# Spreading the source numbers of cold edge chunks by a DMA instead of TensorE, in a four-layer graph kernel

## The reference, cut to what matters

```
x = layernorm(x + segment_sum(w * x[src], dst) @ W0.T)
x = layernorm(x + L1(x))     # two convolutions by degree, batch norms, a product over the joined features
x = layernorm(x + L2(x))     # weighted sums again, two dense products
x = layernorm(x + L3(x))     # a convolution by degree
```

## Time and profile before

| | |
|---|---|
| runs, median (lowest to highest) | 3463.71 us (3461.14 to 3464.36) |
| profiled execution: span | 3458.8 us |
| profiled execution: its own time | not given apart from the span; 4.9 us below the median |
| busy over the span: PE, DVE, ACT, POOL | 82%, 57%, 37%, 71% |
| the first stage, by the first and last POOL scatter of line 1701 | 45.3 to 1256.7 us (starts) |

### The profile page before, as it was taken

The page is one execution under the profiler, slowest core; times in us unless marked ns, Lnnn a source line. Parts: engine busy times, 40 slices in busy tenths (PEclk is TensorE's granted clock), DMA queues, the critical chain, the costliest instruction groups (busy, mean ns, idle before and its releaser), DMA issues. The chain is left out here.

```text
span 3458.8 us, 60258 instructions
## 1 busy us (share of the span) xinstructions
PE 2842.7 (82%) x19203; PEld 2100.9 (61%) x19220; DVE 1983.2 (57%) x6763; ACT 1275.6 (37%) x3485; POOL 2462.4 (71%) x2238
## 2 busy tenths in 40 slices
PE   5989877878888859789977997778888875699995
PEld 4777655656666648444446774366666764466664
DVE  7889777777787729442243434443444564245557
ACT  5566666776877739200010002500111232001123
POOL 3888777786676667577747776777777774777773
PEclk8999998999999979899978997589999998799996
DMA  8787788888888879678856886755556564988884
GB/s 273 112 147 113 142 154 148 155 155 170 179 175 170 180 175 354 180 213 231 237 141 177 226 224 172 217 172 158 162 176 181 159 178 124 297 235 247 252 251 137
DMA packets 658436, 652.79 MB, mean 189 GB/s; under 512 B 87902, under 2 KB 606476, under 8 KB 656588
## 3 DMA queue, kind: packets, MB, share of 16 engines
q0 software_dynamic: 153600, 258.41, 37.3%
q1 hardware_dynamic: 430670, 331.83, 31.2%
q10 hardware_dynamic: 73854, 58.70, 5.4%
HBM read 434.19 MB, written 214.52 MB: 188 GB/s over the span
## 5 line engine op out<-in xcount | busy, mean ns | idle before, releaser
L1701 POOL DMA_INDIRECT A<-rows_buf,big x572 | 902.4, 1578 | 333.8 <-issue 143.5
L882 POOL DMA_INDIRECT rows_buf<-T,idx x888 | 847.7, 955 | 275.9 <-issue 272.2
L976 PE MATMUL PSA<-S,rows_buf 128*128 128x128 bf16 (+2 forms) x5904 | 582.5, 254 | 213.9 <-DMA rows_buf<-X,idx 103.5
L976 PEld LDWEIGHTS PSA<-S,rows_buf 128*128 128x128 bf16 (+2 forms) x5904 | 523.3, 142 | 296.8 <-DMA rows_buf<-X,idx 88.0
L882 POOL DMA_INDIRECT rows_buf<-X,idx x528 | 509.5, 965 | 160.9 <-issue 157.8
L1032 DVE TENSOR_TENSOR accT<-PSA,accT 128x256 f32 (+2 forms) x354 | 132.8, 375 | 835.7 <-PE PSA L976 828.5
L1556 DVE TENSOR_TENSOR accT<-PSA,accT 128x392 f32 (+5 forms) x366 | 239.7, 655 | 173.0 <-issue 59.6
L1394 PE MATMUL PSA<-XRS,rows_buf 128*128 128x256 f32 x1144 | 313.0, 398 | 6.4 <-ACT rows_buf L1406 6.4
L793 ACT ACTIVATE accT<-accT,vec 128x500 f32<-128x500 f32 (+3 forms) x26 | 17.7, 693 | 666.5 <-DVE accT L791 666.4
L1406 ACT ACTIVATE rows_buf<-PSA 128x512 f32<-128x512 f32 x286 | 168.0, 593 | 186.1 <-PE PSA L1394 175.8
L1394 PEld LDWEIGHTS PSA<-XRS,rows_buf 128*128 128x128 f32 x1144 | 209.8, 197 | 32.0 <-ACT rows_buf L1385 6.8
(11 more groups left out here) (315 smaller groups left out, 5805.3 us busy)
## 6 DMA issues: line engine op xcount, KB each, us to landing
XRS<-Ad SPq DMA_DIRECT2D x400, 256.0 KB
Ad<-accT SPq DMA_DIRECT2D x224, 196.0 KB
XRS<-in_xpad SPq DMA_DIRECT2D x192, 128.0 KB, 3.3
Awd<-accT SPq DMA_DIRECT2D x48, 392.0 KB, 3.6
A<-accT SPq DMA_DIRECT2D x9, 1600.0 KB
rows_buf<-T,idx POOLq DMA_INDIRECT x888
rows_buf<-A SPq DMA_DIRECT2D x24, 512.0 KB
accT<-A SPq DMA_DIRECT2D x24, 512.0 KB, 6.1
```

Of the source, the lines that this page charges most:

```text
L882: s_hg[slot(i)][j // 2].on(pool.indirect_dma_start(Gv(slot(i), j), None, table, bass.IndirectOffsetOnAxis(idx[:, c:c + 1], 0)), 16)
L976: last = pe.matmul(PS[bank_of(i)][0:F, W * h:W * h + W], Gv(slot(i), j)[:, o:o + F], hits[:, i % SRING, j, :], start=j + part == 0, stop=j ...
L1701: s_k[n].on(pool.indirect_dma_start(A, bass.IndirectOffsetOnAxis(tgt[:, c:c + 1], 0), G[:, i % RING, j, :], None, compute_op=ALU.add), 16)
```

## The change

The source numbers of each group come as one row of 512 int32 from a new DRAM input `srcrow`, and SP loads it into all 128 partitions with a broadcast transfer (128 times 2 KB). It goes to a ring of three buffers `SR` (SRB = 3), taken from the buffer `junk`, from the space of `srch` and `srcl`, and from the tensor W3, whose weights are loaded after the cold steps. The first three loads are issued after all `zero_copy`; the others stand first in SP's step, three steps ahead, behind a wait for the `equals` that frees the buffer. `equals` does, per chunk, one `scalar_tensor_tensor` that compares, multiplies by `upto` (a bf16 triangle with its diagonal) and writes the row sum. PE's `source_rows`, ACT's `row_sums` and DVE's line 1338 are gone, as are four preparing DVE instructions (lines 439 to 442) and two POOL ones. DVE's `targets(i + 1)` is placed in the middle of step i for all steps.

```diff
-FAR = 16384
+SRB = 3
-    pool.tensor_copy(identb[:, :], ident[:, :])
-    pool.tensor_scalar(lowerb[:, :], lower[:, :], float(FAR), None, ALU.mult)
+    pool.tensor_tensor(upto[:, :], lower[:, :], ident[:, :], ALU.add)
-    link(v.tensor_scalar(tmpi, idx[:, :], 63, None, ALU.bitwise_and))
-    link(v.tensor_copy(srcl, tmpi))
-    link(v.tensor_tensor(tmpi, idx[:, :], tmpi, ALU.subtract))
-    link(v.tensor_copy(srch, tmpi))
...
+        def load_src(i):
+            if i >= SRB:
+                sp.wait_ge(s_eq, i - SRB + 1)
+            g = G0 + i
+            sp.dma_start(SR[i % SRB], a["srcrow"][g:g + 1, :].broadcast_to([128, CG * 128])).then_inc(s_srb[i % SRB], 16)
...
         def transfers(p):
+            if SRB <= p + 1 < NCOLD:
+                load_src(p + 1)
             if 4 <= p < NCOLD:
                 load_x(p)
...
-            v.wait_ge(s_sr, i + 1)
-            v.tensor_tensor(Eq[:, i % 2, :, :], PS[0].rearrange("p (j e) -> p j e", j=CG),
-                            srcf[:, g, :].unsqueeze(2).broadcast_to([128, CG, 128]), ALU.is_equal).then_inc(s_eq, 1)
+            v.wait_ge(s_srb[i % SRB], 16 * (i // SRB + 1))
+            for j in range(CG):
+                last = v.scalar_tensor_tensor(Eq[:, i % 2, j, :], SR[i % SRB][:, 128 * j:128 * j + 128], srcf[:, g, j:j + 1], upto,
+                                              ALU.is_equal, ALU.mult, accum_out=cnt[:, g, j:j + 1])
+            last.then_inc(s_eq, 1)
...
         s_q.by(sp)
         for e in (sc, pool):
             s_cst.by(e)
+        for i in range(SRB):
+            load_src(i)
         transfers(0)
         transfers(1)
-        source_rows(0)
-        source_rows(1)
         weigh(0)
-        row_sums(0)
...
-            if i + 2 < NCOLD:
-                source_rows(i + 2)
...
-            if i + 1 < NCOLD:
-                row_sums(i + 1)
...
+        s_cst.by(v)
         equals(0)
         hot_hits(0)
         scatter_rows()
+        targets(0)
         for i in range(NCOLD):
...
-            if i <= BYACT:
-                targets(i)
...
-            if BYACT < i + 1 < NCOLD:
+            if i + 1 < NCOLD:
                 targets(i + 1)
...
+        sp.wait_ge(s_eq, NCOLD)
+        s_w.on(sp.dma_start(W3[:, :, :], halves(a["L3_gnn_W"])), 16)
```

More of the change, by code:

```diff
@@ L1299, in transfers @@
                     dense_load(sp, t)
[L1301 to L1310, removed]
         def equals(i):
@@ L1316, in equals @@
             v.tensor_tensor(Su[:, i % 2, :, :], iota4, cur16[:, g:g + 1, :].broadcast_to([128, W, CG]), ALU.is_equal).then_inc(s_su, 1)
-            v.wait_ge(s_sr, i + 1)
-            v.tensor_tensor(Eq[:, i % 2, :, :], PS[0].rearrange("p (j e) -> p j e", j=CG),
-                            srcf[:, g, :].unsqueeze(2).broadcast_to([128, CG, 128]), ALU.is_equal).then_inc(s_eq, 1)
[L1321 to L1327, removed]
+            v.wait_ge(s_srb[i % SRB], 16 * (i // SRB + 1))
[3 more added lines that the diff above has]
+            last.then_inc(s_eq, 1)
         def targets(i):
             g = G0 + i
[L1332 to L1337, removed]
-                    last = v.tensor_tensor_reduce(out=junk[:, j, :], in0=Eq[:, i % 2, j, :], in1=lower[:, :], scale=1.0, scalar=0.0,
-                                                  op0=ALU.mult, op1=ALU.add, accum_out=cnt[:, g, j:j + 1])
-                last.then_inc(s_cn, 1)
-                v.wait_ge(s_cn, i + i - BYACT + 1)
-                least = 0.0
-            v.scalar_tensor_tensor(cnt[:, g, :], cnt[:, g, :], least, spare[:, g, :], ALU.is_gt, ALU.mult).then_inc(s_cn, 1)
-            v.wait_ge(s_cn, i + 1 + max(0, i - BYACT + 1))
+            v.wait_ge(s_eq, i + 1)
+            v.scalar_tensor_tensor(cnt[:, g, :], cnt[:, g, :], 1.0, spare[:, g, :], ALU.is_gt, ALU.mult).then_inc(s_cn, 1)
+            v.wait_ge(s_cn, i + 1)
             v.tensor_tensor(tgt[:, CG * g:CG * g + CG], cnt[:, g, :], srcA[:, g, :], ALU.add).then_inc(s_b, 1)
@@ L1845, in spread @@
             sp.dma_start(XR[:, 0, :], a["xpad"][bass.ds(lo, 128), :]).then_inc(s_x[0], 16)
-            pe.wait_ge(s_staged, 1)
+            turned_at = nc.values_load_multi_w_load_instructions(
+                ctl[0:1, 3:4], engines=[ET.SP], min_val=0, max_val=NG - 1, skip_runtime_bounds_check_because="held under NG")[1][0]
+            sp.dma_start(SR[0], a["srcrow"][bass.ds(turned_at, 1), :].broadcast_to([128, CG * 128])).then_inc(s_srb[0], 16)
+            v.wait_ge(s_srb[0], 16)
             for j in range(CG):
-                o = PS[0][:, 128 * j:128 * j + 128]
-                pe.matmul(o, f_h[:, j:j + 1].broadcast_to([128, 128]), identb[:, :], start=True, stop=False)
-                last = pe.matmul(o, f_l[:, j:j + 1].broadcast_to([128, 128]), identb[:, :], start=False, stop=True)
-            last.then_inc(s_sr, 1)
-            v.wait_ge(s_sr, 1)
-            v.tensor_tensor(Eq[:, 0, :, :], PS[0].rearrange("p (j e) -> p j e", j=CG),
-                            f_src.unsqueeze(2).broadcast_to([128, CG, 128]), ALU.is_equal).then_inc(s_eq, 1)
+                last = v.scalar_tensor_tensor(Eq[:, 0, j, :], SR[0][:, 128 * j:128 * j + 128], f_src[:, j:j + 1], upto,
+                                              ALU.is_equal, ALU.mult, accum_out=f_cnt[:, j:j + 1])
+            last.then_inc(s_eq, 1)
             v.wait_ge(s_eq, 1)
-            for j in range(CG):
-                last = v.tensor_tensor_reduce(out=junk[:, j, :], in0=Eq[:, 0, j, :], in1=lower[:, :], scale=1.0, scalar=0.0,
-                                              op0=ALU.mult, op1=ALU.add, accum_out=f_cnt[:, j:j + 1])
-            last.then_inc(s_cn, 1)
+            v.scalar_tensor_tensor(f_cnt, f_cnt, 1.0, f_spare, ALU.is_gt, ALU.mult).then_inc(s_cn, 1)
             v.wait_ge(s_cn, 1)
-            v.scalar_tensor_tensor(f_cnt, f_cnt, 0.0, f_spare, ALU.is_gt, ALU.mult).then_inc(s_cn, 1)
-            v.wait_ge(s_cn, 2)
             v.tensor_tensor(f_tgt, f_cnt, f_srcA, ALU.add).then_inc(s_turn_b, 1)
@@ L1934, in build @@
     s_aw = [nc.alloc_semaphore(f"s_aw{i}") for i in range(2)]
-    s_rs = nc.alloc_semaphore("s_rs")
+    s_srb = [nc.alloc_semaphore(f"s_srb{i}") for i in range(SRB)]
     ABW = [XS[:, 2 + i, :].bitcast(BF16) for i in range(2)]
-    junkA = XS[:, 0:2, :].rearrange("p a b -> p (a b)").rearrange("p (j e) -> p j e", j=CG)
     Eq = Z[:, 0:4, :].rearrange("p a b -> p (a b)").rearrange("p (r j e) -> p r j e", r=2, j=CG)
     Ms = Z[:, 4:8, :].rearrange("p a b -> p (a b)").rearrange("p (r n) -> p r n", r=2)
-    junk = Z[:, 8:10, :].rearrange("p a b -> p (a b)").rearrange("p (j e) -> p j e", j=CG)
+    SR = [ap.bitcast(I32) for ap in (Z[:, 8:10, :].rearrange("p a b -> p (a b)"), part[4][:, 0:512], W3[:, :, :].rearrange("p k n -> p (k n)"))]
     spread()
@@ L2379, in by_chunk @@
         return full.reshape(n, 128).T
+    given["srcrow"] = np.concatenate([given["src"], np.zeros(128 * NG * CG - E, given["src"].dtype)]).reshape(NG, 128 * CG)
     given["src"] = by_chunk(given["src"], NG * CG, 0)
```

28 lines of the change are left out of this document (10 added, 18 removed).

## The result

The changed kernel takes 3530.14 us (median of 4 runs, 3526.07 to 3539.01), the kernel before, run beside it, 3462.43 us (3458.26 to 3464.36): a ratio of 1.0207 [1.0193, 1.0222]. It is slower by some 68 us; the prediction said 3461 and at most 3507. The profiled execution took 3539.01 us, its span is 3537.8.

What follows compares the result with a forecast made beforehand. It took the first stage as bound by PE early, mutual DVE and PE waits in the middle, and SP's window parts late. Terms +30 - 10 - 13 - 9 made -2: 3461 us as a run, no tellable change; range 3424 to 3507.

Steps and rivals of the forecast that it cites:

- Part 1, the start: Start of first stage: the first source row lands behind the zeroing, so step 4's tables come 30 us late (28 to 34).
- Part 2, the compare: DVE, each step: four compares with row sums take 0.87 us instead of 0.60, +0.27; net -0.69 in the last 51 steps.
- The rival with the dear compare (1.3 us): DVE, steps 4 to 93: four compares at 1.3 us cost 0.7 per step, kernel 3491 us; chance 0.07.
- Part 3, PE: PE, each step: twelve matmuls go, saving 0.67 us.
- part 4, ACT: ACT, 92 steps: four row sums go, 1.2 us per step, and with them DVE's 13.0 us of waits for them.
- the -10 of steps 4 to 22: PE-bound steps 4 to 22: 18 steps at 0.67 us less some given back by DVE's +0.27, a gain of 10 us.
- Part 5, SP and the DMA engines: 143 loads of 256 KB cost SP about 1.0 us per step (0.4 to 2.3); slower scatters cost nothing while POOL has slack.
- -9 in the last stretch: Steps 94 to 142: 46 loads add 46 us to SP's occupied time, so 415 us against 424, a gain of 9.
- the formula of the prediction: Last stretch, SP-bound: it takes 364 + 5 + 46c us, c being SP's us per step for a load.
- SP's queue is the price: Last stretch: loads standing before window parts in SP's step cost c = 2.0 us each, +37, kernel 3507 us; chance 0.20.

Runs made afterwards that it cites:

- e1: The changed kernel with its first three source loads issued before the zeroing instead of behind it; ratio 1.0099 to the kernel before.
- e11: The kernel of e9 with each of DVE's four compare-and-count instructions issued twice, the copies unread; ratio 1.0237 to the kernel before.
- e9: The changed kernel without source loads in the cold steps: PE makes the rows in two matmuls a chunk, DVE compares from PSUM; 3441.06 us, ratio 0.9942.
- e10: The kernel of e9 with ACT's four row sums put back, unread, in the first 92 steps, and DVE's wait for them; ratio 1.0213.
- e8: The kernel of e9 with the first matmul of each chunk issued twice, so twelve matmuls a step again; ratio 0.9999 to the kernel before.
- e2: The changed kernel with the loads from the fourth on issued by ACT's queue at the end of its step; ratio 1.0196 to the kernel before.
- e7: The kernel of e9 with the 256 KB loads put back on SP's queue at their place, read by nobody; ratio 1.0141 to the kernel before.
- e12: The kernel of e7 with the unread loads ended at step 93; ratio 0.9991 to the kernel before.
- e5: The changed kernel unaltered, run again as a yardstick; 3532.5 us, ratio 1.0217 to the kernel before.
- e3: The changed kernel with int16 source rows, 128 KB a load in the same number of packets; ratio 1.0087 to the kernel before.
- e6: The changed kernel with the first three loads ahead of the zeroing and int16 source rows; ratio 1.0041 to the kernel before.

## Why the prediction was wrong

The sum was +30 - 10 - 13 - 9 = -2; the profiled spans gave +79.0. The miss of 81 us is 4 at the start, 27 in steps 4 to 93, 53 in the last stretch, and -3 behind it.

**Part 1, the start: right.** +34.0 at the end of its range (28 to 34), by the mechanism given: first compare at 62.44 (61 to 63 foreseen) behind a wait of 40.03. e1 takes 24 us of it back.

**Part 2, the compare: mis-sized.** 1.09 us for the four, not 0.87; the pitch is 0.27, not the 0.21 of line 1338. The term is +0.49 a step, not +0.27, and e11 shows that DVE's time counts up to step 94, in full from step 22 on. The prediction let a good part of it be hidden by waits for PE. 0.22 by 90 steps is 20 us of the 27 by which steps 4 to 93 missed their forecast; the loads' 8.5 to 10 us (below) are of the size of the rest. The rival with the dear compare (1.3 us) was no nearer than the forecast: 1.09 lies 0.21 below the one and 0.22 above the other. The rule of the Trainium skill that stood with it ("Vector Engine (DVE) Microarchitecture Reference", section 7, half rate with two sources in SBUF that are not bf16) has no case here: 345 ns from SBUF with int32 and 344 from PSUM with f32 in e9. The Trainium skill, the same page, section 5.2, gives one column a cycle, 1.0417 ns, and some 75 ns for each instruction; from that I estimate 0.21 us for 128 columns. The row sums of line 1338 kept to it; this instruction with its accumulator takes 0.06 more.

**Part 3, PE, and part 4, ACT: hidden in one sum.** The -10 of steps 4 to 22 did not come (-1.6): PE's busy time there fell from 140.4 of 141 us to 130.9 of 139 and DVE's rose from 120.9 to 128.9, so PE stopped being the bound and its relief bought nearly nothing. Without transfers (e9) the steps from 22 to 94 take 583.2 us against 591.8, with DVE's 0.49 by 72, 35 us, paid in them. So the relief of ACT and PE and the early `targets` are worth some 44 us there. That is worked out from e9 and e11 and not run by itself; how much each has of it stays open, as e10 measured the sums in another place than the old one. Four matmuls of the twelve are worth 6 to 20 us (e8).

**Part 5, SP and the DMA engines: the step that failed.** "So about 1.0 us of SP per step", with the scatters' share ("I cost this at nothing while POOL has slack"), and -9 in the last stretch: it was +44. By the formula of the prediction, SP was occupied for 469 us less its 15 us of waits for others, 454, which is 364 + 46c with c = 1.95. So in this stretch the outcome is near that of the rival "SP's queue is the price" with c = 2.0 (+44 against +37), but not by its mechanism: off SP's queue the loads cost nearly the same (e2). The whole kernel lies 23 us above that rival's 3507, as the steps before missed their forecast too. A load took 0.82 to 0.98 us of all 16 DMA engines (e7 less e12; the queue's share), not the 0.62 that its bytes take at the 423 GB/s of the earlier trace rows. And in this stretch a share of 0.84 was not room. The prediction looked at the 0.71 of the first steps alone and gave POOL's slack as the reason for a cost of nothing, and it called SP's waits for window parts a matter of SP. They were the time of the DMA engines, which the scatters and the window parts share: with the loads, POOL, SP, ACT and DVE all wait longer for transfers. That the lower clock of TensorE, which came with the loads, has no part in it is not shown (e12). By these runs the +44 has two parts: the loads' time, 32 to 38 us (e7 less e9, e7 less e12), and DVE's wait for rows that land late, net 12 to 16 us (after and e5 less e7). Together they are more than 44; the relief elsewhere gives some 3 to 9 us back (before less e9, before less e12).

In steps 22 to 94 the same loads cost 8.5 us (e7 less e9) to 10 (e12 less e9), at a DMA share of 0.81 before and 0.88 after: 0.13 us each. DVE is the bound there (e11).

## What to carry to other kernels

Before work is moved from an engine to transfers, look at the DMA share of each stretch and at who waits for landings: here a stretch at 0.84 to 0.88, in which engines already waited for landings, grew by about the DMA time of every load, on SP's queue and on ACT's, while steps 22 to 94, bound by DVE, took the same loads almost for nothing. Cost a transfer by what such transfers take of the 16 engines beside the others (share by span, over their number), not by its bytes at the best rate. And a small load that the first steps need belongs ahead of the bulk transfers of the start.

The best kernel of this study takes only the other half of the change: the compare that counts, and no row sums on ScalarE, with the rows still made by TensorE in two matmuls a chunk (e9, 0.9942 [0.9928, 0.9956] of the kernel before).

## What the runs showed of the hardware

A broadcast load of one 2 KB row to 128 partitions added 0.98 us of all 16 DMA engines to its queue's time (256 KB in 0.98 us are 267 GB/s) and 0.82 us to a stretch whose transfers were its limit. Halving its bytes, with the same 128 packets, took back 31 us in the last stretch, 0.67 us a load, the reader's waits among them (after less e3; 28 to 32 by e5 and after less e6). The loads cost some 48 us there in all (after less e9), so the bytes cost more than the number of packets.

SP stood 8.69 us on the issue of a single load, behind the zeroing, and 3.3 us on each of the next two. SP's timeline of the changed kernel:

```profile
41.18 0.32 SPq L1205 DMA_DIRECT2D A<-accT  x1
41.55 8.69 SPq L1240 DMA_DIRECT2D rows_buf<-in_srcrow  x1
50.28 3.26 SPq L1240 DMA_DIRECT2D big<-in_srcrow  x1
53.58 3.31 SPq L1240 DMA_DIRECT2D W<-in_srcrow  x1
```

The median over all these loads is 0.43 us. Behind the zeroing the issue itself held SP, though not for every transfer: the last part of the zeroing, issued just before, took 0.32 us.

TensorE's mean granted clock in the last stretch was 0.98 with four matmuls a step fewer and no loads (e12), as before, and 0.93 with the loads beside the same matmuls (e7), where PE waited 88 us for others instead of 68. With the loads and eight matmuls fewer still it was 0.89 (after); which share the fewer matmuls have in that is open.

DVE's compare with a row sum of 128 columns has the same pitch, 0.27 us, from int32 (after), from int16 (e6) and from PSUM in f32 (e9).
